# Four-deep store buffers of a selective-scan kernel: one DMA semaphore per buffer in place of a wait ahead of each GpSimd store

## The reference, cut to what matters

```python
xn   = layernorm(x)
proj = xn @ W_in.T                      # 4192 columns: x_s 2048, z 2048, B 16, C 16, dt 64
x_s, z, B_s, C_s, dt = split(proj)
u    = silu(conv1d(x_s, 4 taps, causal) + conv_b)
dt   = softplus(dt @ W_dt.T + b_dt)     # 2048 columns
h[t] = exp(dt*A) * h[t-1] + dt*B_s*u    # for each of 2048 channels and 16 states
y    = sum_n h*C_s + u*D
y    = y * silu(z)
out  = layernorm(xn + y @ W_out.T)*ln_g + ln_b
x    = x + out + (xn @ CB.T)*(SCB/127) + bias
```

## Time and profile before

| | us |
|---|---|
| median of two runs | 6600.79 |
| lowest and highest | 6579.66, 6621.91 |
| the profiled execution | 6631.35 |
| its span on the slowest core (core 6) | 6629.8 |
| spans of the other cores | 6549.2 to 6605.0 |

### The profile page before, as it was taken

How to read it: one execution, slowest core, us unless ns; L and a number is a source line. 1 busy time by engine, 2 the same in 40 slices (tenths; PEclk the granted TensorE clock), 3 DMA queues, 4 the chain that set the end, 5 groups by cost and what they waited for, 6 DMA issues and landing times.

```text
span 6629.8 us, 28358 instructions; the slowest of 8 cores (6549.2 to 6629.8 us)
## 1 busy us (share of the span) xinstructions
PE 2110.5 (32%) x6224; PEld 705.9 (11%) x6224; DVE 4486.2 (68%) x2252; ACT 1717.4 (26%) x1485; POOL 574.1 (9%) x1069
## 2 busy tenths in 40 slices
PE   0029534554211222222222222222222222245554
PEld 0013211111000000000000000000000000012221
DVE  2630222211341999999999999999999999934454
ACT  0222333333444222222222222222222222210000
POOL 1112232233322000000000000000000000000000
PEclk9997656666555555555555555555555555567777
DMA  8552344344444444434444443444344344343332
GB/s 268 180 176 99 111 121 117 106 120 126 121 121 147 159 176 171 185 151 171 171 164 172 171 184 152 171 176 184 146 174 180 152 172 181 128 123 94 100 100 86
DMA packets 377917, 996.00 MB, mean 150 GB/s; under 512 B 201650, under 2 KB 219187, under 8 KB 298803
## 3 DMA queue, kind: packets, MB, share of 16 engines
q1 hardware_dynamic: 312644, 785.25, 34.5%
q0 software_dynamic: 65104, 208.93, 8.5%
HBM read 768.33 MB, written 208.86 MB: 147 GB/s over the span
## 4 chain that ended last, share of the span: by engine, by line
DVE 52%; issue 15%; DMA 13%; PE 10%; SPq 5%; ACT 4%; POOL 1%; DVEq 1%; ACTq 0%; POOLq 0%
DVE p_h L778 34%; DVE p_X L771 8%; PE pY L519 6%; SPq L81 3%; DMA h_dtu<-p_dtu 3%; DMA h_Bbc<-p_bc 3%; PE pY L933 2%; SPq L75 2%; DVE p_acc L659 2%; DMA h_Cbc<-p_bc 2%; DMA p_x<-x 1%; DVE p_yg L810 1%; DMA h_xs<-p_ev 1%; DMA h_WinTb<-p_ot 1%; PE pY L824 1%
## 5 line engine op out<-in xcount | busy, mean ns | idle before, releaser
L778 DVE TENSOR_TENSOR_SCAN p_h<-p_dA,p_X 128x4096 bf16<-128x4096 f32 x256 | 2225.0, 8691 | 53.4 <-ACT p_dA L756 27.4
L824 PE MATMUL pY<-p_hC,identb 128*128 128x512 bf16 x2048 | 901.9, 619 | 2795.8 <-DVE p_hC L789 2795.8
L756 ACT ACTIVATE p_dA<-p_dtn,A_pos 128x4096 f32<-128x4096 bf16 x256 | 949.5, 3709 | 2678.4 <-DVE p_h L778 2101.3
L519 PE MATMUL pY<-p_xt,p_w 128*128 128x512 bf16 (+2 forms) x2240 | 566.6, 422 | 470.2 <-DMA p_xt<-h_xnb 463.6
L824 PEld LDWEIGHTS pY<-p_hC,identb 128*128 128x128 bf16 x2048 | 262.9, 137 | 3434.4 <-issue 3434.4
L789 DVE TENSOR_TENSOR p_hC<-p_h,p_bcC 128x4096 bf16<-128x4096 bf16 x256 | 586.8, 2292 | 27.3 <-DVE p_h L778 0.9
L771 DVE TENSOR_TENSOR p_X<-p_dtu,p_bcB 128x4096 bf16<-128x4096 bf16 x256 | 584.9, 2285 | 28.5 <-DMA p_bcC<-h_Cbc 28.5
L651 DVE TENSOR_SCALAR p_acc<-p_xs,convw 128x512 f32<-128x512 f32 x128 | 61.7, 482 | 689.3 <-ACT p_u L589 668.0
L933 PE MATMUL pY<-p_wout,p_yg 128*128 128x512 bf16 x1024 | 301.2, 467 | 352.1 <-DMA p_x<-x 322.2
L75 POOL DMA_DIRECT2D h_yg<-p_yg x16 | 8.5, 532 | 3678.4 <-DVE p_yg L810 3426.5
L519 PEld LDWEIGHTS pY<-p_xt,p_w 128*128 128x128 bf16 (+2 forms) x2240 | 234.0, 106 | 801.8 <-issue 705.0
(11 more groups left out here) (91 smaller groups left out, 1942.8 us busy)
## 6 DMA issues: line engine op xcount, KB each, us to landing
p_bcB<-h_Bbc SPq DMA_DIRECT2D x256, 1024.0 KB, 6.1
p_bcC<-h_Cbc SPq DMA_DIRECT2D x256, 1024.0 KB, 8.3
p_x<-x SPq DMA_DIRECT2D x64, 512.0 KB, 4.4
h_xs<-p_ev POOLq DMA_DIRECT2D x128, 256.0 KB, 2.6
p_xs<-h_xs SPq DMA_DIRECT2D x128, 256.0 KB, 3.5
p_sg<-WinT SPq DMA_DIRECT2D x8, 2096.0 KB, 15.5
h_xn<-p_xn POOLq DMA_DIRECT2D x32, 512.0 KB, 4.8
h_sz<-p_evb POOLq DMA_DIRECT2D x128, 128.0 KB, 2.2
```

The source lines that it names most:

```text
L519: ins = tensor.matmul(ps[0:M, :], p2_w[:, k * OUTF + c0:k * OUTF + c0 + M], p2_xt[:, off + k * WIN:off + (k + 1) * WIN], start=(k == 0), s ...
L756: ins = scalar.activation(out=p6_dA[:, (n % 2) * L:(n % 2 + 1) * L], in_=p6_dtn[:, jo:jo + L], func=AF.Exp, scale=A_pos[:, j * NS + n:j * ...
L778: ins = vector.tensor_tensor_scan(out=p6_h[:], data0=p6_dA[:, nb:nb + L], data1=p6_X[:], initial=0.0, op0=ALU.mult, op1=ALU.add)
L824: ins = tensor.matmul(psl(s), identb[:], p6_hC[:, nb + s * 512:nb + (s + 1) * 512], start=(n == 0), stop=(n == NS - 1))
```

## The change

Parts 3, 4 and 5 get one semaphore for each of their four buffers, in place of two that alternate, and the `front` wait ahead of each of their stores is gone. Six semaphores are new; one that nobody used (`so`) is dropped. The barriers and the last wait of the program walk all semaphores, so they get six more each.

```diff
-                "qT0", "qT1"]
-    S = {n: 0 for n in ["sv", "sa", "sp", "so"] + DMA_SEMS}
+                "qG8", "qG9", "qG10", "qG11", "qG12", "qG13", "qT0", "qT1"]
+    S = {n: 0 for n in ["sv", "sa", "sp"] + DMA_SEMS}
...
-                                    if not counting:
-                                        front(gpsimd, ("qG%d" % (2 + i3 % 2),))
-                                    dma(gpsimd, "qG%d" % (2 + i3 % 2),
+                                    dma(gpsimd, "qG%d" % (2, 3, 10, 11)[i3 % 4],
                                         h_u[j * 128:(j + 1) * 128, w3 * WIN:(w3 + 1) * WIN],
...
-                                    qq = "qG%d" % (4 + i4 % 2)
-                                    if not counting:
-                                        front(gpsimd, (qq,))
+                                    qq = "qG%d" % ((4, 5, 12, 13)[i4 % 4])
                                     dma(gpsimd, qq,
...
-                                    if not counting:
-                                        front(gpsimd, ("qG%d" % (6 + G5 % 2),))
-                                    dma(gpsimd, "qG%d" % (6 + G5 % 2),
+                                    dma(gpsimd, "qG%d" % (6 + G5 % 4),
                                         dst[n * 128:(n + 1) * 128, w5 * WIN:(w5 + 1) * WIN],
```

## The result

| | before | after |
|---|---|---|
| median, us | 6591.45 | 6457.31 |
| lowest to highest | 6569.37 to 6621.91 | 6417.82 to 6480.42 |
| cores of the profiled execution, us | 6549.2 to 6629.8 | 6399.6 to 6428.5 |

The ratio after to before is 0.9783, with a 95% interval of 0.9753 to 0.9814: the kernel is 2.2% faster, and since the interval reaches past 0.98, whether it is more than 2% is not settled. By the medians that is 134 us, by the ratio 143. The forecast was a gain of 193 us and 6408 us; the time lies in the stated range, and on the slow side of the forecast.

What follows compares the result with a forecast made beforehand. The joint stage was taken as bound by latencies, ScalarE waiting for stores. Part 5's 155 us plus part 4's 38 us made 193 us, giving 6408 us in terms of the runs' median of 6600.8; range 6350 to 6490 us.

Steps and rivals of the forecast that it cites:

- What bounds the kernel, and where the gain lies: Joint stage, 380 to 2120 us: bound by latencies, no engine full; all gain comes from there, the scan stays.
- Part 3 at nothing, barriers under 1 us: Part 3's silus: their 20.4 us of store waits yield nothing; six more semaphores at barriers cost under 1 us.
- Part 4, 38 us: Logarithms of part 4: third and fourth waits of each half shrink, 44 us less 6 for later first landings.
- Part 5's quiet pace, 0.84 us: Part 5's casts: a buffer's round of 3.37 us yields four stores, so 0.84 us each instead of 1.345.
- Part 5's first half: Start of each part 5, beside SyncE's loads: 10 us taken off the 165 us gain for longer landings.
- cast 4: Fifth cast of each part 5 window, waiting for store 0: 3.5 us forecast, with 1.8 and 6 as ends.
- the first rival: Part 5: landings grow with depth, pitch (L + 1.2)/4; at L = 3.2 us 58 us lost, 6466 us; chance 0.14.
- that rival: Part 4 doesn't gain, DMA engines being full: 38 us go, cast 4 waits 6 us, 6466 us; chance 0.10.
- other wait took the place: Rival at GpSimd: slower issue or little room with several stores queued, pace stays 1.345 us, 6580 us; chance 0.05.
- The slower case: Part 5: landings over L = 4.5 us make the deeper queue cost time; at 6.95 us about 6740 us; chance 0.03.
- The PSUM pace: Part 5's upper case: TensorE and ScalarE trading PSUM banks at 0.69 us per cast, 34 us more, 6374 us; chance 0.10.
- The stage's end: Sign to check: the joint stage should end near 1930 us, with the scan still taking 3780 us.

Runs made afterwards that it cites:

- the kernel with parts 3 and 4 alone: Changed kernel with part 5 given back its two alternating semaphores and `front` wait; parts 3 and 4 keep the change: 6550.55 us, ratio 0.9938.
- thinned kernels: Transposes of windows 2 on carry 128 of 512 rows, part 3's loads 16 columns: changed kernel 6387.46 us, kernel before 6547.46 us, one run each.
- VectorE's three steps: Three of four convolution instructions per block left out, against the changed kernel with SyncE's loads thinned: 6201.95 us in one run.
- eight-buffer kernels: Changed kernel with eight buffers and semaphores instead of four: in part 5 alone 6366.16 us, ratio 0.9657; in parts 4 and 5 6306.29 us, ratio 0.9583.
- the kernel with all the edits but the last: Changed kernel plus eight buffers in parts 4 and 5, transposes issued earlier and four PSUM banks for part 5: 6289.94 us, ratio 0.954.

## Why the prediction was right, and where it was not

**What bounds the kernel, and where the gain lies: right.** The stage shortened, the scan stood still, and ScalarE's idle time in the two lines explains the spans to within 1 us (both over several cores).

**Part 3 at nothing, barriers under 1 us: right.** The silus' idle time is 210.8 us before and after.

**Part 4, 38 us: right, position by position.** On core 7, the sums over sixteen halves of the waits of the first and second logarithm that wait are 72.4 and 14.5 us, and of the third and fourth 9.2 and 9.0; on core 6 before they were 70.4, 11.7, 41.1 and 20.4. So the waits that `front` never held stay, and the other two fall from 61.5 to 18.2 us. The 6 us that the sum took off for later landings of the first store of a half didn't show: the first two waits come to 78.7 us before and 77.0 after over eight cores. One half on ScalarE's timeline, which answers to the earlier trace rows:

```profile
861.90 1.41 ACT L606 ACTIVATE p_dtn<-p_sig,cns 128x512 bf16<-128x512 f32 x2 [5.19 <-DMA h_dtu<-p_dtu]
864.53 0.72 ACT L606 ACTIVATE p_dtn<-p_sig,cns 128x512 bf16<-128x512 f32 x1 [1.22 <-DMA h_dtu<-p_dtu]
865.46 0.72 ACT L606 ACTIVATE p_dtn<-p_sig,cns 128x512 bf16<-128x512 f32 x1 [0.21 <-DMA h_dtu<-p_dtu]
```

The saving came out at 38 us by the time of the kernel with parts 3 and 4 alone, and at 45 us by the eight cores' rows of the whole.

**Part 5's quiet pace, 0.84 us: right, to 0.06 us.** ScalarE's timeline in the second half of a part 5:

```profile
736.27 1.32 ACT L617 CAST p_bc<-pY 128x512 bf16<-128x512 f32 x2 [0.51 <-DMA h_Cbc<-p_bc]
737.76 1.32 ACT L617 CAST p_bc<-pY 128x512 bf16<-128x512 f32 x2 [0.17 <-DMA h_Cbc<-p_bc]
739.55 0.59 ACT L617 CAST p_bc<-pY 128x512 bf16<-128x512 f32 x1 [0.47 <-DMA h_Cbc<-p_bc]
740.31 0.59 ACT L617 CAST p_bc<-pY 128x512 bf16<-128x512 f32 x1 [0.18 <-DMA h_Cbc<-p_bc]
```

From 736.27 to 739.55 four casts take 3.28 us, where the round of a buffer had been put at 3.37. Over all cores and windows the last twelve casts of a part 5 go at 0.90 us each. Landings there are 2.2 us as forecast. The fit of the Trainium skill ("DMA: Bandwidth & Descriptors", Anatomy of one DMA) gives 2.3 us for this size, as an estimate; by that rule, the trace agrees within 0.1 us in this stretch, where the DMA engines' share is 0.43.

**Part 5's first half: the step that failed.** The sum took 28 casts at 0.84 us, 3.5 us for cast 4, and 10 us in all for the traffic at the beginning, and the casts were to have 80 to 110 us of idle time; they have 136 to 157, by core. ScalarE's and then the chain's rows of one window (start us, us, what) show what happens instead:

```profile
894.20 1.05 ACT L617 CAST p_bc<-pY 128x512 bf16<-128x512 f32 x2
895.63 1.07 ACT L617 CAST p_bc<-pY 128x512 bf16<-128x512 f32 x2 [0.38 <-PE pY L543]
901.89 1.07 ACT L617 CAST p_bc<-pY 128x512 bf16<-128x512 f32 x2 [5.18 <-DMA h_Bbc<-p_bc]
...
908.82 1.07 ACT L617 CAST p_bc<-pY 128x512 bf16<-128x512 f32 x2 [2.32 <-DMA h_Bbc<-p_bc]
910.28 1.07 ACT L617 CAST p_bc<-pY 128x512 bf16<-128x512 f32 x2 [0.38 <-PE pY L543]
913.62 0.59 ACT L617 CAST p_bc<-pY 128x512 bf16<-128x512 f32 x1 [2.27 <-DMA h_Bbc<-p_bc]
```
```profile
898.14 5.81 DMA h_Bbc<-p_bc
...
905.35 3.58 DMA h_Bbc<-p_bc
...
910.63 4.32 DMA h_Bbc<-p_bc
...
919.43 2.19 DMA h_Cbc<-p_bc
```

Landings run 5.81, 3.58, 4.32 us, and only then 2.19. Over the 64 windows of the eight cores, from their timelines:

| per window, us | before | forecast | after |
|---|---|---|---|
| first `h_Bbc` store issued behind the end of cast 0 | 5.7 | about 2 | 2.0 |
| its landing | 4.1 | 2.2 to 5 | 6.05 |
| wait of cast 4 | 7.95 | 3.5 | 6.19 |
| the 28 casts | 39.4 | 24.85 | 27.6 |
| of them, the first 14, each | 1.51 | about 0.93 | 1.10 |

Cast 4 is mis-sized by 2.7 us, eight times: 22 us. The 28 casts by 2.8 us, eight times: 22 us. Together 44 us, and 155 less 44 is 111, where 108 was measured; the other 3 us are what core 6, from which the sum took its time before, lies above the mean of the cores. That is the whole of the difference, and the mechanism is that of the first rival, landings that grow with depth, for half of each part 5. The first `h_Bbc` store is issued 3.7 us sooner, as forecast, but takes 1.9 us longer to land: half of what the change took out of GpSimd's waits went into the landing. For the casts behind cast 4, the rival's formula (L + 1.2)/4 gives 1.13 us with L = 3.3 us, the median landing of all sixteen `h_Bbc` stores on cores 0 and 3, and 1.05 us with the 3.0 us of the stores from the fifth on; 1.10 was measured. I had it as a case of its own for all 224 casts, when it held for half of them beside a quiet second half. The Trainium skill ("DMA: Bandwidth & Descriptors", Latency and other measured facts) has the receipt from HBM cost more at high load. By that rule L would have been 4.0 us, as an estimate; the trace agrees in the direction (2.6 us with lighter loads, 3.0 to 3.6 with all of them), not in the size.

Two faults of working led to it. I put the stretch's traffic into the new sum at 10 us, by a guess of ten casts at 0.1 to 0.15 us, although the old sum held the measured price of the same traffic: the thinned kernels put it at 31 us before and 34 after. And I took it that cast 4 would wait little once GpSimd had caught up. GpSimd has caught up, as its timeline in that window shows:

```profile
896.02 0.54 POOL L75 DMA_DIRECT2D h_dtu<-p_dtu  x1
896.55 2.13 POOL L75 DMA_DIRECT2D h_Bbc<-p_bc  x4
```

The first `h_Bbc` store is issued at 896.55, straight behind part 4's last. But cast 4, which waits for it, goes only at 901.89, 5.3 us later, in a stretch in which the DMA engines' share is 1.03 (895 to 904 us, against 0.43 from 733 to 742, in the windows above). The prediction's "2.2 to 5 us" for this landing ended short of the ordinary case (6.05 us in the mean); the landings of 5.44 and 6.95 us in the earlier trace rows and the full DMA engines in the earlier trace rows had shown what to expect there.

**The other rivals.** Part 4 gained, so that rival falls. GpSimd took no longer to a store with four in flight (548 ns mean of one, 543 before), and the quiet pace was met, so no other wait took the place. The slower case needed landings over 4.5 us throughout; they were 3.0 to 3.6 for half of the stores. Its sum was also wrong: at L = 4.5 us the pitch of 1.43 us gives 6408 + 224 x 0.59 = 6540 us, still faster than before, because the gains of cast 4 and part 4 stay in that sum. The PSUM pace came only with eight buffers. The stage's end, forecast near 1930 us, was met at 1923, but by luck, with the help of the slower TensorE on the core that the page of before shows; without it, it would have been missed by the same 42 us as the spans (151 us in place of 193).

**What stays open.** Even thinned, the first half goes at 0.95 us per cast and cast 4 waits 4 us. VectorE's three steps aren't the cause. That the stores of part 4 still in flight are (theory E) fits the eight-buffer kernels, in which `h_Bbc` lands later the more stores stand ahead of it. No run took part 4's stores away, but two windows come near it. In the first, no store of part 4 is ahead and only loads (with the last stores of part 3) run beside part 5: cast 4 waits 4.4 us, and 2.6 us thinned. In the last, there are no transposes and no loads of part 3 (four of part 4 are left), and part 4's stores are ahead: it waits 5.1 us, and 5.0 thinned. In windows 1 to 5 both are there, and it waits 6.8 to 7.6 us (means of eight cores). So each of the two seems to hold cast 4 by itself; but window 6, with part 4's stores ahead and part 3's loads beside, has 3.5 us only. E is supported and not shown.

## What to carry to other kernels

A wait of the issuing engine for its own stores can be struck when the buffers' owner waits too; a store then costs the round of a buffer over the number of buffers, and with four buffers that formula held to about 0.06 us, given the landing. Take the landing from the stretch in question, neighbours and backlog included, and not from the quietest row of the trace, and expect it to grow there when more stores are in flight. And when the sum for before comes from measured rows and the sum for after from a model, any cost that only the measured side holds is booked as a gain. And when a wait of one engine is taken out, look at what the engines behind it have ready: with eight buffers in both parts, ScalarE came to part 5 before its input had been loaded.

## What the runs showed of the hardware

- A 128 KB store that GpSimd issues lands in 2.2 us in quiet stretches at four in flight as at two, and in 2.5 to 3.7 us at eight. With the core's own loads beside it, it takes 2.2 to 2.5 us at two in flight, 3.0 to 3.6 at four and 4.3 to 5.8 at eight (medians of the cores).
- The cost to this path of the loads that were thinned is about the same with two stores in flight (31 us) as with four (34 us).
- From the landing of a store to the start of the cast that waits for it pass 0.08 us, in every window of the changed kernel.
- In one execution two cores of eight ran the same matmuls at 422 ns where the others took 386 to 388, with a granted clock of 0.64 to 0.65 in the stage against 0.67, and ended 19 to 81 us behind them. It is no property of the kernel before: cores 4 and 5 of the kernel with all the edits but the last took 427 and 428 ns in one execution, the others 385 to 387. Compare medians over runs, or the same row on all cores, and not the profiled core alone.
